# A GNN kernel's edge sort: one gather of 384 keys per bucket, decoded in 16-bit words, and batch-norm factors computed between turns of the sort

## The reference, cut to what matters

```python
for i in range(3):                                   # the first network
    agg = segment_sum(h[src], dst, num_segments=N)
    h = relu(_bn((h + agg) @ W1[i] + b1[i], g[i, 0], be[i, 0], rm[i, 0], rv[i, 0]))
    h = relu(_bn(h @ W2[i] + b2[i], g[i, 1], be[i, 1], rm[i, 1], rv[i, 1]))
def _bn(h, gamma, beta, mean, var):
    return (h - mean) * (gamma * rsqrt(var + BN_EPS)) + beta
```

## Time and profile before

| | |
|---|---|
| time, median of three runs | 4071.94 us |
| the profiled execution's own time | 4071.28 us |
| its span | 4069.2 us |
| busy in the span: PE, DVE, ACT, POOL | 3723.1, 3125.1, 2450.5, 1342.8 us |
| sort network | 0 to 247.9 us |
| from the sorted keys to the fill's first instruction | 247.9 to 289.2 us |
| fill | 289.2 to 537.4 us |
| layers | 537.4 to 4069.2 us |

### The profile page before, as it was taken

The page is one execution under the profiler, slowest core; times in us unless marked ns, Lnnn a source line. Parts: engine busy times, 40 slices in busy tenths (PEclk is TensorE's granted clock), DMA queues, the critical chain, the costliest instruction groups (busy, mean ns, idle before and its releaser), DMA issues.

```text
span 4069.2 us, 59937 instructions
## 1 busy us (share of the span) xinstructions
PE 3723.1 (91%) x17037; PEld 2913.9 (72%) x17037; DVE 3125.1 (77%) x5676; ACT 2450.5 (60%) x4604; POOL 1342.8 (33%) x1941
## 2 busy tenths in 40 slices
PE   0118889999999999999899999999999999999999
PEld 0116678888888644555688888888888888888887
DVE  9989956677687778887668767877876876786685
ACT  1119966656656787787565555555555555566655
POOL 0021135534545310000362343244244234446624
PEclk9999999999999999999899999999999999999999
DMA  2019964545543322221144454444444444434444
GB/s 64 0 45 367 365 218 136 158 137 144 156 128 108 93 70 75 71 66 55 52 115 119 117 142 130 120 136 133 121 132 138 119 118 140 122 98 111 117 133 136
DMA packets 320608, 509.09 MB, mean 125 GB/s; under 512 B 118979, under 2 KB 187324, under 8 KB 319895
## 3 DMA queue, kind: packets, MB, share of 16 engines
q1 hardware_dynamic: 299484, 452.24, 38.7%
q0 software_dynamic: 7856, 46.93, 3.2%
q10 hardware_dynamic: 12938, 6.05, 0.7%
HBM read 396.99 MB, written 43.87 MB: 108 GB/s over the span
## 4 chain that ended last, share of the span: by engine, by line
PE 50%; issue 0%; ACT 0%; DVE 0%; POOL 0%; ACTq 0%; POOLq 0%
PE ps L2224 41%; PE ps L2340 3%; PE ps L2341 3%; PE ps L2342 1%; PE ps L2343 1%; PE ps L2370 0%; PE ps L2256 0%; PE ps L2326 0%; PE ps L2365 0%; PE ps L2262 0%; PE ps L2247 0%; ACT wide L2063 0%; PE ps L2239 0%; PE ps L2381 0%; PE ps L2191 0%
## 5 line engine op out<-in xcount | busy, mean ns | idle before, releaser
L2224 PE MATMUL ps<-wide,hi 128*128 128x512 f32 (+2 forms) x5537 | 2148.9, 390 | 19.8 <-issue 9.5
L2224 PE MATMUL ps<-wide,lo 128*128 128x512 f32 (+2 forms) x5537 | 2076.5, 379 | 0.0
L2063 DVE CAST wide<-ring 128x1536 fp32r<-128x1536 uint8 (+2 forms) x1274 | 1311.5, 1029 | 492.5 <-PE ps L2224 486.9
L2224 PEld LDWEIGHTS ps<-wide,hi 128*128 128x128 f32 x5537 | 1041.8, 188 | 224.5 <-issue 29.8
L2224 PEld LDWEIGHTS ps<-wide,lo 128*128 128x128 f32 x5537 | 1043.6, 188 | 188.7
L2063 ACT CAST wide<-ring 128x768 fp32r<-128x768 uint8 (+1 forms) x1274 | 1152.8, 905 | 3.7 <-DMA ring<-count 2.9
L2433 ACT CAST hi<-high 128x128 fp32r<-128x128 f32 x1274 | 380.7, 299 | 1038.2 <-PE ps L2224 623.4
L2162 POOL TENSOR_TENSOR lo<-hN,high 128x128 fp32r<-128x128 f32 x686 | 561.5, 822 | 750.5 <-PE ps L2224 437.7
L2162 POOL TENSOR_TENSOR lo<-hB,high 128x128 fp32r<-128x128 f32 x588 | 494.1, 841 | 752.6 <-PE ps L2224 495.3
L2220 PE MATMUL ps<-hN,hB 128*128 128x512 f32 (+1 forms) x1274 | 525.3, 569 | 5.6 <-DVE aggT L2396 4.2
L2426 ACT ACTIVATE hN<-aggT,source_scores 128x512 f32<-128x512 f32 (+1 forms) x637 | 428.9, 695 | 118.0 <-PE ps L2220 86.9
(11 more groups left out here) (246 smaller groups left out, 3403.2 us busy)
## 6 DMA issues: line engine op xcount, KB each, us to landing
ring<-count SPq DMA_DIRECT2D x490, 320.0 KB, 3.0
ring<-count SPq DMA_DIRECT2D x441, 256.0 KB, 2.7
ring<-count SPq DMA_DIRECT2D x490, 224.0 KB, 2.6
wide<-aggT POOLq DMA_DIRECT2D x49, 896.0 KB, 6.2
count<-aggT SPq DMA_DIRECT2D x49, 800.0 KB, 4.0
hB<-mid SPq DMA_DIRECT2D x192, 32.0 KB, 1.9
hN<-mid SPq DMA_DIRECT2D x192, 32.0 KB, 1.9
hB<-squares SPq DMA_DIRECT2D x96, 32.0 KB, 2.1
```

The lines of the kernel that those rows point to most:

```text
L2063: return copy(wide[:, g % WIDE_SLOTS, c0:c1].rearrange("p (t u f) -> p t u f", u=2, f=P), rows[:, g % row_slots, c0:c1].rearrange("p (t f ...
L2224: ins = e.matmul(ps[:, c, 0:size], part[:, g % CUT_SLOTS, :], wide[:, g % WIDE_SLOTS, w0:w0 + size], start=k == 0 and part is hi, stop=k = ...
```

## The change

- **Gather.** The ten gathers of 256 keys and the ten of 129 become ten gathers of 384 keys (`WINDOW`), from the tile in which the bucket starts. The passes that find the exact first key are gone. The tile count is done in three groups of columns (4, 4, 2), each in four independent passes without a running sum (PE adds the four up), and the gathers of a group wait only for their group.
- **Fold.** DVE flips each window's bits by xor with the bucket's number, so that keys of the bucket become numbers below 2^15 and all others are larger, and takes the minimum of the three thirds of 128, cut off at `ABSENT` = 2^15. The result is a float.
- **Decode.** ACT copies the transposed columns to 16-bit words, and DVE decodes with three `tensor_scalar` and one `scalar_tensor_tensor` in 16-bit words for each of the three groups. `row_of` and `orders_by` become uint16 and hold the mark `ABSENT` for no key.
- **Statistics.** `bn_aggr` is replaced by five operations 49 wide on all blocks. The `measure` calls move by three blocks.
- **Batch-norm factors.** The same operations as before (two reciprocals and what follows) are cut into 14 steps, one in each gap of the last seven sort rounds. ACT's two square roots for them move ahead of its copies; DVE waits for them before the first of these rounds.
- **The flag `many`** comes from counting the marks in `row_of` at the end of the fill: DVE counts 1280 words a partition, PE sums with a matrix of ones, DVE compares, then does the four final additions.

```diff
-            for g in range(FREE // TILE):
-                ... # tiles_before[:, :] (+)= start_row > first, 1280 wide, each waits for the one before
+            def count_tiles(c0, c1):
+                for g in range(FREE // TILE):
+                    e.tensor_scalar(tiles_before[:, g, c0 * P:c1 * P], start_row[:, c0 * P:c1 * P].bitcast(F32), A[1][:, g * TILE:g * TILE + 1],
+                                    None, ALU.is_gt).then_inc(ch.sem, ch.up())
+                before_at.append(ch.n)
+            def name_tiles(n):
+                c0, c1 = COLUMN_GROUPS[n]
+                e.wait_ge(s["total"], n + 1)
+                e.tensor_scalar(tile_f[:, c0:c1], ps[:, 5 + n, c0:c1], -1.0, 0.0, ALU.add, ALU.max).then_inc(ch.sem, ch.up()); e.wait_ge(ch.sem, ch.n)
+                e.tensor_copy(tile_i[:, c0:c1], tile_f[:, c0:c1]).then_inc(ch.sem, ch.up())
+                tile_at.append(ch.n)
+            count_tiles(*COLUMN_GROUPS[0])
+            count_tiles(*COLUMN_GROUPS[1])
+            name_tiles(0)
+            count_tiles(*COLUMN_GROUPS[2])
+            name_tiles(1)
+            name_tiles(2)
...
+            def fold(c):
+                whole = windows[:, c, :].bitcast(I32)
+                part = [windows[:, c, i * P:(i + 1) * P] for i in range(WINDOW // P)]
+                e.wait_ge(s[f"window{c}"], 16)
+                e.tensor_scalar(whole, whole, flip_col[:, c:c + 1], None, ALU.bitwise_xor).then_inc(ch.sem, ch.up()); e.wait_ge(ch.sem, ch.n)
+                e.tensor_tensor(part[1], part[0].bitcast(I32), part[1].bitcast(I32), ALU.min).then_inc(ch.sem, ch.up()); e.wait_ge(ch.sem, ch.n)
+                e.scalar_tensor_tensor(part[0], part[2].bitcast(I32), float(ABSENT), part[1], ALU.min, ALU.min).then_inc(s["folded"], 1)
+            def decode(n):
+                ...
+                e.wait_ge(s["kcopied"], n + 1)
+                e.tensor_scalar(place[:, cols], keys[:, cols], 1, (P - 1) << 8, ALU.logical_shift_left, ALU.bitwise_and).then_inc(ch.sem, ch.up())
+                e.tensor_scalar(odd_half[:, cols], keys[:, cols], 14, 1, ALU.logical_shift_right, ALU.bitwise_and).then_inc(ch.sem, ch.up())
+                e.tensor_scalar(row_of[:, cols], keys[:, cols], ABSENT + P - 1, None, ALU.bitwise_and).then_inc(ch.sem, ch.up())
+                e.wait_ge(ch.sem, ch.n)
+                e.scalar_tensor_tensor(code_of[:, cols], odd_half[:, cols], 255.0, place[:, cols], ALU.mult, ALU.add).then_inc(ch.sem, ch.up())
+            for c in range(BG // 2):
+                fold(c)
             e.wait_ge(s["rooted"], 3)
+            net.rsqrt(ch, inv, var, root[:, :], off)
+            ...
+            fold(5), fold(6), decode(0), fold(7), fold(8), fold(9), decode(1), decode(2)   # in this order, one a line
...
@@ gpsimd
+            for n, (c0, c1) in enumerate(COLUMN_GROUPS):
+                e.wait_ge(s["dve"], tile_at[n])
+                for c in range(c0, c1):
+                    e.indirect_dma_start(out=windows[:, c, :], out_offset=None,
+                                         in_=keys_dram.rearrange("(t l) -> t l", l=TILE),
+                                         in_offset=bass.IndirectOffsetOnAxis(ap=tile_i[:, c:c + 1], axis=0))\
+                        .then_inc(s[f"window{c}"], 16)
...
@@ the seven last rounds
-                measure(range(8 * n, 8 * n + 4))
+                measure(range(8 * n - 3, 8 * n + 1))
+                factor_work(ch, 2 * n)
...
-                measure(range(8 * n + 4, 8 * n + 8))
+                measure(range(8 * n + 1, 8 * n + 5))
+                factor_work(ch, 2 * n + 1)
...
@@ fill_counts, vector, behind the 49 blocks
+            e.memset(ones, 1.0).then_inc(s["absent"], 1)
+            e.tensor_scalar(junk, row_of[:, :], float(ABSENT), 0.0, ALU.is_ge, ALU.add, accum_out=absent[:, 0:1]).then_inc(s["absent"], 1)
+            e.wait_ge(s["added"], 1)
+            e.tensor_scalar(many, ps[:, TURN, P:P + 1], float(BG * P * P - E) + 0.5, None, ALU.is_gt)
@@ fill_counts, tensor, last
+            e.wait_ge(s["absent"], 2)
+            e.matmul(ps[:, TURN, P:P + 1], ones, absent[:, :], start=True, stop=True).then_inc(s["added"], 1)
@@ build_counts
-        row_of, code_of = sb("row_of", [P, BG * P], BF16), sb("code_of", [P, BG * P], I16)
-        orders_by = sb("orders_by", [P, P, NCHUNK], BF16)
+        row_of, code_of = sb("row_of", [P, BG * P], U16), sb("code_of", [P, BG * P], I16)
+        orders_by = sb("orders_by", [P, P, NCHUNK], U16)
```

More of the change, by code:

```diff
@@ L219, in sort_edges @@
     names = ["id0", "cst", "pad", "x", "w", "v", "wturned", "wkept", "orders", "edges", "dve", "turned", "copied", "kout",
-             "lists", "total", "kturned", "kcopied", "over", "rooted"] + [f"{n}{c}" for n in ("tile", "slot") for c in range(BG)]
+             "lists", "total", "kturned", "kcopied", "rooted", "folded"] + [f"window{c}" for c in range(BG)]
     with ExitStack() as tmp, stage(nc, *names) as (block, s):
@@ L242, in sort_edges @@
         tile_i = sb("tile_i", [P, BG], U32)
[L243 to L255, removed]
+        windows = net.hN[:, 0:BG * WINDOW].rearrange("p (c l) -> p c l", l=WINDOW)
+        c0 = BG * WINDOW
+        keys, place, odd_half = (net.hN[:, c0 + n * BG * P // 2:c0 + (n + 1) * BG * P // 2].bitcast(U16) for n in range(3))
         stats = sb("stats", [P, NB, 6])
-        mv = sb("mv", [P, NB, 2])
+        moments = sb("moments", [P, 4, NB])
+        twice_mean, apart, both, var = (moments[:, n, :] for n in range(4))
         root = sb("root", [P, NB])
         turns = [k for k in range(LOG_FREE + 1, 18)]
-        lists_at, ready, sorted_at, before_at, tile_at, first_at, spread_at = [], [], [], [], [], [], []
+        lists_at, ready, sorted_at, before_at, tile_at, spread_at = [], [], [], [], [], []
         @block.vector
@@ L364, in _ @@
             sorted_at.append(ch.n)
-            for g in range(FREE // TILE):
[L367 to L373, removed]
-                e.wait_ge(ch.sem, ch.n)
@@ L375, in _ @@
[L375 to L391, removed]
@@ L393, in _ @@
-            e.wait_ge(s["rooted"], 3)
[L394 to L418, removed]
@@ L422, in _ @@
+            for c in range(BG // 2):
+                fold(c)
+            e.wait_ge(s["rooted"], 3)
+            net.rsqrt(ch, inv, var, root[:, :], off)
+            e.scalar_tensor_tensor(off, twice_mean, -0.5, inv, ALU.mult, ALU.mult).then_inc(ch.sem, ch.up())
+            fold(5)
+            fold(6)
+            decode(0)
+            fold(7)
+            fold(8)
+            fold(9)
+            decode(1)
+            decode(2)
             e.wait_ge(ch.sem, ch.n)
@@ L518, in _ @@
                 .then_inc(s["lists"], 1)
+            e.wait_ge(s["v"], 16 * (len(vectors) + len(directs)))
+            for out, v in roots:
+                e.activation(out, v, ACT.Sqrt, bias=net.eps[:, 0:1]).then_inc(s["rooted"], 1)
             for n, k in enumerate(turns):
@@ L553, in fill_counts @@
     assert len(pieces) == groups == 4
-    names = ["left", "apart", "right", "mm", "out", "spread", "normal", "turned", "state", "high", "hi", "lo", "summed", "whole", "copied",
+    names = ["left", "apart", "right", "mm", "out", "spread", "normal", "turned", "state", "high", "hi", "lo", "summed", "whole", "copied", "absent", "added",
              *[f"loaded{j}" for j in range(EARLY_SLOTS)]]
```

148 lines of the change are left out of this document (81 added, 67 removed).

## The result

The changed kernel takes 4062.36 us (median of 9 runs, 4059.95 to 4062.93) against 4072.37 us before (median of 9): a ratio of 0.9973, 95% interval 0.9964 to 0.9982, 10.0 us faster. A second set of runs gave 4061.2 against 4072.63. Forecast were 14.0 us. The direction held; the time lies 0.14 us inside the upper end of the range, and 4.0 us of the forecast gain are missing (2.6 in the second set).

A forecast was written before the change was run, and what follows sets the result against it. POOL's unbroken row of twenty gathers was taken to bound the 41.3 us stretch between sort and fill; -15.7 there and +1.7 at the fill's end make -14.0 us, 4057.9 us, range 4053.5 to 4062.5.

The forecast's parts named there:

- The gathers: POOL behind the sort: first gather at 252.5, tenth starting 11.57 us later, plus 0.7 us of contention with the folds.
- Rival 1: Gathers behind the sort each wait for a whole xor of the folds: 2.6 us later, 4060.5 us; chance 0.11.
- rival 3: Gathers bound by their bytes, so the pitch grows with window size: 5.6 us more, 4063.5 us; chance 0.04.
- Landing: Each 1536-byte window lands 3.1 us (2.9 to 3.6) after its gather starts; the first is there at 255.9.
- DVE behind the gathers: Folds of 0.98 us and decodes of 1.33 us end the stage at 272.3 against 287.97, 15.7 us saved.
- The factors between turns: Fourteen factor steps fit DVE's idle gaps in the sort: 0 us; under 6 us if nothing fitted.
- The fill's masks: In the fill, `left` comparing uint16 instead of bf16 keeps its pace: no change, 0 us.
- Rival 2: The fill's uint16 comparison leaves the two-a-cycle pace: 1.6 us a block more, 78 us, 4136 us; chance 0.04.
- The flag at the fill's end: Four final additions stand behind a wait for PE's last matmul: 1.7 us lost (1.2 to 2.2); the count is free.

The follow-up runs named there:

- e8: Changed kernel with the fold's xor as a two-input tensor_tensor, column broadcast, instead of the one-source form: 4063.09 us.
- e6: Changed kernel with all 14 batch-norm factor steps back behind the sort, ahead of the first fold: 4064.43 us.
- e9: Changed kernel with all ten gathers waiting for the last group's tile number: 4063.06 us.
- e7: Kernel before with only the factors put between the sort's turns, and the statistics and roots moved: 4074.18 us, ratio 1.0002.
- e2: Changed kernel with the flag's comparison moved behind the four additions: 4058.72 us.
- e3: Changed kernel with the last block's transfer into `wide` replaced by a cast on DVE, flag still ahead of the additions: 4056.79 us.
- e11: Changed kernel with ten added transfers of 128 x 1024 bytes on POOL's queue early in the sort: 4061.47 us.
- e12: Changed kernel with five added transfers of 128 x 1024 bytes on POOL's queue early in the sort: 4060.66 us.
- e10: Changed kernel with DVE counting the marks only once the last block's transfer has landed: 4060.92 us.
- e4: Changed kernel with a DVE cast for the last block's transfer and the flag's comparison behind the additions: 4055.14 us, 0.9955 of the kernel before.
- e5: Changed kernel with 20 unneeded transposes on PE while it waits for the last transfer: 4060.74 us.

## Why the prediction was right, and what failed in it

- **The gathers.** Forecast: tile_i at 251.6, first gather 252.5, tenth 264.8. Measured: 251.28, 252.22, 264.21. Five of the ten gathers cost 0.07 to 0.10 us more, one 0.03; between the first start and the tenth this made 0.4 us, for 0.7 taken. By e8 this is for the most part the one-source xor. Rival 1 (a whole xor for each) and rival 3 (bound by bytes) are out: from the second gather on the pitch stayed at 1.25 to 1.36 us for windows of 1.5 times the size.
- **Landing.** Forecast 3.1 us, first window at 255.9; the first fold started at 255.48, 3.26 us behind the first (longer) gather, and the median of the ten landings in the DMA view is 3.1.
- **DVE behind the gathers.** Fold 0.98 against 0.99 measured, decode 1.33 against 1.33, end of the stage 272.3 against 271.89. The saving of this part was forecast at 15.7 us and is 16.1. That DVE and not the last landing is late at the end was right; e6 and e9 show that both lie close together: DVE's work delayed by 4.4 costs 3.1, POOL's by 2.0 costs 2.2.
- **The factors between turns.** 0 forecast, 0 measured: the idle time before the turn after four bn_stats fell from 0.38 to 0.18 us and the turn did not start later (sort's end 247.75 for 247.89). What the prediction said of their place, that they cost nothing beside twenty gathers, e7 shows. It did not say, and e6 shows, that beside ten they would cost 3.1.
- **The fill's masks.** No change forecast; a block still takes 4.77 us (`left` starts at 499.36 and 504.13 in the trace after, and takes 1.89 us). Rival 2 is out.
- **The flag at the fill's end: the step that was mis-sized.** It was put at 1.7 us and the stage lost 5.0. The wait of the additions, the mechanism I had named, is 1.6 us by the rows and 1.9 by the fill of e2. What I left out is that the end of the fill hangs on the last transfer into `wide`, and that I took its landing as given: the earlier trace rows show PE's last product, not what it had waited for. The landing came 1.9 us later, PE's idle time of 2.35 us became 4.2, and PE's granted clock fell to the lower level as its last eight products began, 1.5 us more. e3 takes the transfer away and wins 6.7 us of fill, more than the 3.4, since it removes also the wait that the kernel before has. How much of the 1.5 us comes from the longer wait is open: in e7 the wait was the old one and the clock fell all the same, 1.1 us after PE had resumed, which cost 0.7 us.
- **Luck.** The time fell inside the range by 0.14 us. The upper end had been put there for late gathers, which did not come; what filled it was the end of the fill, to which the prediction gave at most 0.5 us above its 1.7.

**What stays open** is why the landing is late. In the four traces in which I read all 49 landings (e8, e9, e11, e12) they mostly run through a pattern, falling by about 0.7 us from block to block (7.5, 6.8, 6.1, 5.5) and starting over. The last one comes at 5.5 us in the two traces of kernels with the old sort end and the old fill (before, e7) and at 7.3 to 7.5 us in all ten traces of changed kernels that have this transfer. The counting beside it (e10), the fill's start, which varied from 273.4 to 276.5 (e6, e9), and the number of transfers before it (e11, e12) are excluded. The instructions added at the fill's end or the 16-bit tables were not tried.

The traces hold a strong candidate that no run moves: the loading of the program's own instructions. The DMA view of the 5 us from the last transfer's issue shows, after the change, one 16 KB and one 8 KB transfer of instructions (queues q8 and q14; packets, MB, share of 16 engines), and before none:

```profile
q8 instruction: 1, 0.02, 1.3%
q14 instruction: 1, 0.01, 1.0%
```

It is so in all ten traces with the late landing and in neither of the two with 5.5 us. After the change the transfer's last packets then trickle in, 14 of them from 516.6 to 518.3 us:

```profile
DMA packets 14, 0.07 MB, mean 36 GB/s; under 512 B 4, under 2 KB 4, under 8 KB 14
```

Before, all that is left 4.9 us behind the issue is 16 packets of under 512 bytes. The store of the counts that SP issues at the same time lands late too, 5.3 us for 3.4. And of the 196 landings of the four traces 48 take 7.2 us or more: 42 of them have a 16 KB instruction transfer within 5 us of their issue, of the other 148 only 14. So the change may have done no more to the landing than to move the moment at which instructions are loaded. That is a coincidence in time, not a cause shown: no run shifts the loads and leaves the rest alone.

## What to carry to other kernels

When two gathers in a row on one queue become one, price the queue first and then every engine that had free time beside it: work that cost nothing before (the factors) has to find another gap in the same change. And where the change adds an instruction to the end of a stage, look at what that end waits for, and at the idle time of TensorE in it: here a wait that grew by 1.9 us came with 1.5 us of products at the lower clock, and a last transfer that nothing else covers made the end depend on when it landed. Doing the last piece on an idle engine (e3, e4) took both away.

## What the runs showed of the hardware

- A `scalar_tensor_tensor` on 16-bit operands had no faster pace: 0.69 us for 512 columns, as with 32-bit ones, while the 16-bit `tensor_scalar` took 0.28 for 512.
- A 384-wide xor on DVE lengthened a gather on POOL by up to 0.10 us. Three of the xors that began beside a gather in e9 took 0.54 to 0.67 us for 0.42, others beside one 0.41; that the gather lengthened them was not tested:

```profile
258.82 0.63 DVE L393 TENSOR_SCALAR hN<-hN,flip_col 128x384 int32<-128x384 int32 x1
```

- When the granted clock fell differed from execution to execution by more than 3 us. Of the ten traces in which the last transfer landed late, seven have the fall inside PE's wait, 0.7 us (e10) to 2.3 us (e8) before the first of the eight products; in the other three it came 0.2 us (after), 0.6 us (e12) and 0.8 us (e5, whose transposes had cut the idle time to 2.0 us) behind that product's start. Of the two traces with an idle time of 2.35 us one keeps the full clock for all eight products (before), in the other it falls 1.1 us behind their start (e7).
- Late landings of the fill's transfers coincide with the loading of instructions: 42 of 48 landings of 7.2 us or more in e8, e9, e11 and e12 had a 16 KB instruction transfer within 5 us of their issue, 14 of 148 others.
